# Graph-network chain on one core: the block stage's one-hots written as 32-bit rounded floats, its weights split in two parts

## Time and profile before

| | us |
|---|---|
| median of three runs | 2580.64 |
| the profiled execution's own time | 2578.91 |
| its span, first to last instruction | 2577.2 |
| TensorE matmul busy | 2291.4 (89%) |
| VectorE busy | 1690.3 (66%) |
| ScalarE busy | 922.8 (36%) |
| GpSimd busy | 1375.3 (53%) |
| mean granted TensorE clock, of full speed | 0.88 |

### The profile page before, as it was taken

The page is one execution under the profiler, slowest core; times in us unless marked ns, Lnnn a source line. Parts: engine busy times, 40 slices in busy tenths (PEclk is TensorE's granted clock), DMA queues, the critical chain, the costliest instruction groups (busy, mean ns, idle before and its releaser), DMA issues.

```text
span 2577.2 us, 38097 instructions
## 1 busy us (share of the span) xinstructions
PE 2291.4 (89%) x7759; PEld 1176.1 (46%) x7759; DVE 1690.3 (66%) x4905; ACT 922.8 (36%) x2623; POOL 1375.3 (53%) x1706
## 2 busy tenths in 40 slices
PE   5789088727779999999998999999999999999997
PEld 3457067616655554454444333333333333333335
DVE  8973389939970421104136888888888888888885
ACT  0010077727760000000103444444444444444444
POOL 3886777776666666566504444444444444444440
PEclk7666555656669999999998999999999999999999
DMA  5212100011121211111102333333333333333331
GB/s 194 53 34 50 6 7 2 2 15 15 15 50 23 50 17 15 51 15 15 47 0 92 89 87 86 86 86 86 86 86 86 86 86 86 86 86 86 86 85 40
DMA packets 77939, 146.95 MB, mean 57 GB/s; under 512 B 28688, under 2 KB 41221, under 8 KB 77517
## 3 DMA queue, kind: packets, MB, share of 16 engines
q0 software_dynamic: 51200, 103.93, 17.6%
q1 hardware_dynamic: 23746, 37.13, 4.4%
q10 hardware_dynamic: 2946, 5.28, 0.6%
HBM read 122.74 MB, written 22.82 MB: 56 GB/s over the span
## 4 chain that ended last, share of the span: by engine, by line
PE 70%; POOL 15%; DVE 7%; issue 5%; DMA 2%; DVEq 1%; ACT 0%; ACTq 0%; SPq 0%; POOLq 0%
PE ps L747 25%; POOL pair_table L446 15%; PE ps L735 13%; PE ps L550 10%; PE ps L575 7%; PE ps L736 4%; PE ps L692 3%; PE ps L637 2%; PE ps L719 1%; DVE dense L1108 1%; DVE adj_t L1130 1%; DMA pair_table<-dense 1%; DVE dense L1107 1%; PE ps L669 1%; PE ps L727 1%
## 5 line engine op out<-in xcount | busy, mean ns | idle before, releaser
L747 PE MATMUL ps<-adj_t 128*128 128x512 f32 x1408 | 670.7, 609 | 0.0
L458 POOL DMA_INDIRECT src_table<-st_rec,st_idx x320 | 386.4, 1208 | 273.3 <-DMA st_rec<-records 181.2
L446 POOL DMA_INDIRECT pair_table<-dense x320 | 395.2, 1235 | 150.4 <-issue 96.6
L505 POOL DMA_INDIRECT adj_t<-z_table,adj_t x352 | 340.6, 968 | 182.3 <-issue 85.1
L927 ACT ACTIVATE adj_t<-adj_t 128x128 f32<-128x128 f32 x1056 | 343.3, 388 | 257.6 <-DVE adj_t L1275 257.6
L735 PE MATMUL ps<-wring,adj_t 128*128 128x512 f32 x704 | 371.8, 610 | 2.9 <-DVE adj_t L1249 2.9
L747 PEld LDWEIGHTS ps<-adj_t 128*128 128x128 f32 x1408 | 246.6, 190 | 251.0 <-issue 242.0
L636 PE MATMUL ps<-dense 128*128 128x128 bf16 x512 | 147.0, 287 | 188.4 <-DVE adj_t L1130 119.6
L637 PE MATMUL ps<-dense 128*128 128x128 f32 x1024 | 303.7, 434 | 0.0
L637 PEld LDWEIGHTS ps<-dense 128*128 128x128 f32 x1024 | 249.5, 299 | 19.5
L861 ACT ACTIVATE dense<-dense 128x128 f32<-128x128 bf16 x512 | 157.2, 307 | 248.9 <-DVE dense L1108 238.5
(11 more groups left out here) (208 smaller groups left out, 3083.3 us busy)
## 6 DMA issues: line engine op xcount, KB each, us to landing
src_table<-dense SPq DMA_DIRECT2D x8, 704.0 KB, 7.0
adj_t<-src_table SPq DMA_DIRECT2D x88, 64.0 KB, 1.8
adj_t<-z_table,adj_t POOLq DMA_INDIRECT x352, 3.6
pair_table<-dense POOLq DMA_INDIRECT x320, 2.6
src_table<-st_rec,st_idx POOLq DMA_INDIRECT x320, 2.6
records<-dense SPq DMA_DIRECT2D x1, 5000.0 KB
st_rec<-records POOLq DMA_DIRECT2D x80, 62.5 KB, 2.2
wring<-in_edge_attr SPq DMA_DIRECT2D x2, 1562.5 KB
```

The costliest lines, as they stand in the source:

```text
L446: g.indirect_dma_start(out=pair_tables[h], out_offset=bass.IndirectOffsetOnAxis(ap=rows_i[h][0:EP, j:j + 1].bitcast(u32), axis=0), in_=pai ...
L458: g.indirect_dma_start(out=src_table, out_offset=bass.IndirectOffsetOnAxis(ap=st_idx[0:EP, k, c:c + 1].bitcast(u32), axis=0), in_=st_rec[0 ...
L505: g.indirect_dma_start(out=zg[:, s, c, :], out_offset=None, in_=z_table, in_offset=bass.IndirectOffsetOnAxis(ap=dsti[:, s, c:c + 1].bitcas ...
L747: last = mm(bank[6 + h], oh[:, c, :], msg[:, c, h * D:(h + 1) * D], start=c == 0, stop=c == GROUP - 1)
```

## The change

The type of the four operands of the block products becomes float32r, a 32-bit float rounded for TensorE. VectorE writes both one-hots in it, from the same bf16 row of numbers. The weight of a record is split into a rounded part and the rest, once for each part of the edges, by two chained VectorE instructions after the wait for the table; the rest takes the place of the record's fourth word. ScalarE makes two scaled copies of the destination's one-hot, by the rounded weight and by the rest, and copies the source's one-hot no more. TensorE makes one product of 256 columns (A, and W with the rounded weight) and one of 128 that is accumulated onto W. The ring `sel` takes 4096 words of `dense` where the two before took 3072, and `dense_r` is the same memory as `dense`.

```diff
-        sel_b = dense[:, 0:2 * AB * P].bitcast(bf16).rearrange("p (c k n) -> p c k n", k=2, n=P)
-        sel_f = dense[:, 2 * AB * P:6 * AB * P].rearrange("p (c k n) -> p c k n", k=2, n=P)
+        sel = dense_r[:, 0:8 * AB * P].rearrange("p (c k n) -> p c k n", k=4, n=P)
+        HI_AT = PAIR_AT + PAIR_CHUNKS * PAIR_COLS
+        w_hi = dense_r[:, HI_AT:HI_AT + PAIR_CHUNKS].rearrange("p (h c) -> p h c", h=PARTS)
...
-                    mm(bank[c][:, 0:P], sel_b[:, c, 0, :], sel_b[:, c, 1, :], start=True, stop=True)
-                    mm(bank[c][:, P:2 * P], sel_f[:, c, 0, :], sel_f[:, c, 1, :], start=True, stop=True).then_inc(blk_done, 1)
+                    mm(bank[c][:, 0:2 * P], sel[:, c, 0, :], sel[:, c, 1:3, :].rearrange("p k n -> p (k n)"), start=True, stop=False)
+                    mm(bank[c][:, P:2 * P], sel[:, c, 0, :], sel[:, c, 3, :], start=False, stop=True).then_inc(blk_done, 1)
...
-                    A(sel_f[:, c, 0, :], sel_b[:, c, 0, :], ACT.Copy)
-                    A(sel_f[:, c, 1, :], sel_b[:, c, 1, :], ACT.Copy, scale=dense[:, ds(n * PAIR_COLS + (PAIR_AT + 2), 1)]).then_inc(selw_ready, 1)
+                    A(sel[:, c, 2, :], sel[:, c, 1, :], ACT.Copy, scale=dense_r[:, ds(n + HI_AT, 1)].bitcast(f32))
+                    A(sel[:, c, 3, :], sel[:, c, 1, :], ACT.Copy, scale=dense[:, ds(n * PAIR_COLS + (PAIR_AT + 3), 1)]).then_inc(selw_ready, 1)
...
-            dve.wait_ge(pair_in[0], 16)
+            def split_weights(h):
+                dve.wait_ge(pair_in[h], 16)
+                rec = pair_sb[:, h, :].rearrange("p (c w) -> p c w", w=PAIR_COLS)
+                link(v.tensor_copy(w_hi[:, h, :], rec[:, :, 2]))
+                link(v.tensor_tensor(rec[:, :, 3], rec[:, :, 2], w_hi[:, h, :], ALU.subtract))
+
+            split_weights(0)
...
-                v.tensor_scalar(sel_b[:, c, 0, :], iotab[:, :], dense[:, ds(col, 1)], None, ALU.is_equal)
-                v.tensor_scalar(sel_b[:, c, 1, :], iotab[:, :], dense[:, ds(col + 1, 1)], None, ALU.is_equal).then_inc(sel_ready, 1)
+                v.tensor_scalar(sel[:, c, 0, :], iotab[:, :], dense[:, ds(col, 1)], None, ALU.is_equal)
+                v.tensor_scalar(sel[:, c, 1, :], iotab[:, :], dense[:, ds(col + 1, 1)], None, ALU.is_equal).then_inc(sel_ready, 1)
...
-                    dve.wait_ge(pair_in[p], 16)
+                    split_weights(p)
```

More of the change, by code:

```diff
@@ L72, in build @@
           l2_w, l2_b, w_in_s, w_in_v, wf1, bf1, wf2, bf2, w1_s, w1_v, w2_s, w2_v, out):
-    f32, bf16, i32, u32 = mybir.dt.float32, mybir.dt.bfloat16, mybir.dt.int32, mybir.dt.uint32
+    f32, f32r, bf16, i32, u32 = mybir.dt.float32, mybir.dt.float32r, mybir.dt.bfloat16, mybir.dt.int32, mybir.dt.uint32
     ALU, ACT, AX = mybir.AluOpType, mybir.ActivationFunctionType, mybir.AxisListType
@@ L94, in build @@
         adj = adj_t[:, :].rearrange("p (k n) -> p k n", k=2)
-        dense = sb("dense", [P, NT * D + 2 * KT * N])
+        with nc.sbuf_tensor("dense", [P, NT * D + 2 * KT * N], f32) as dense:
+            pass
+        dense_r = sb("dense_r", [P, NT * D + 2 * KT * N], f32r)
         xb = dense[:, 0:NT * D].rearrange("p (t n) -> p t n", t=NT)
@@ L167, in build @@
         st_rec = sb("st_rec", [P, 2, 4 * SRC_COLS])
-        sel_b = dense[:, 0:2 * AB * P].bitcast(bf16).rearrange("p (c k n) -> p c k n", k=2, n=P)
-        sel_f = dense[:, 2 * AB * P:6 * AB * P].rearrange("p (c k n) -> p c k n", k=2, n=P)
+        sel = dense_r[:, 0:8 * AB * P].rearrange("p (c k n) -> p c k n", k=4, n=P)
+        HI_AT = PAIR_AT + PAIR_CHUNKS * PAIR_COLS
+        w_hi = dense_r[:, HI_AT:HI_AT + PAIR_CHUNKS].rearrange("p (h c) -> p h c", h=PARTS)
+        assert HI_AT + PAIR_CHUNKS <= 10 * 1024
         assert KT * N <= PJ * BUCKETS[0] // 2
```

## The result

The changed kernel takes 2584.47 us (median of 12 runs, 2582.36 to 2587.88). The kernel before, run beside it, takes 2581.16 (12 runs, 2577.28 to 2582.25). The ratio is 1.0018 with a 95% interval of 1.0009 to 1.0026: 3.3 us slower, where 2.2 had been worked out. The profiled execution took 2583.92 us.

What follows compares the result with a forecast made beforehand. Part two of the block stage was taken as paced by VectorE's streams, then its sequencer, then TensorE. 8.4 - 6.8 + 1.0 - 0.4 = +2.2 us gave 2581.1 against the profiled time, 2583 as a median, range 2574 to 2608.

Steps and rivals of the forecast that it cites:

- The slack of part one: Part one of the block stage: 43 us of waiting for the scatter's second table, so changes up to that cost nothing.
- The selects: VectorE's one-hot writes in part two: 33 ns longer each, exposed in half the chunks, +8.4 us, ends 0 and +16.9.
- The hiding of the other half: Third add to next half's first add: streams of 1.45 us stay below the sequencer's 1.47 and 1.82, costing nothing.
- Rivals 3 and 4: Part two: selects cost nothing more, -6.2 us, chance 0.10; or nothing hides and nothing comes back, +18 us, chance 0.15.
- Rival 2: VectorE's selects fall to one element a cycle for the new type, +27 us, 2608; chance 0.07.
- TensorE: Block products at bf16's price, 0.53 us a chunk at most, give back 0.21 us an iteration in part two: -6.8 us.
- Rival 1: TensorE becomes the bound if the narrow product costs f32's four passes: eight passes a chunk, +25 us, 2607; chance 0.18.
- ScalarE: Two scaled copies a chunk in part two, 0.58 us where it has 0.72, hidden behind VectorE, costing nothing.
- Rival 5: GpSimd's transfers in part two hold the longer selects up once more each, +28 us, 2609; chance 0.04.
- the sign of 6.19 us for an iteration: Expected sign that the forecast was right: part two's iterations go from 6.14 to 6.19 us.
- The split: VectorE's copy and subtraction on the weight before part two's first chunk: +1.0 us, ends 0.8 and 2.
- The tail: TensorE's last four chunks after the last select, before the last adds: -0.4 us, ends -0.8 and +0.5.

Runs made afterwards that it cites:

- relief kernel: Kernel before, with only the weighted product and its scaled and plain copies in the rounded type, weight's rest left out, selects still bf16: 2574.0 us, ratio 0.9969.
- silent kernel: Kernel before, with GpSimd's scatter for layer four held back until the block stage is over: 2692.89 us, part two's iterations 6.139 us.
- bf16 kernel: Changed kernel's plan with split weight, two scaled copies and two products, but all block operands in bf16: 2575.48 us, ratio 0.9976 to the kernel before.
- silent changed kernel: Changed kernel, with GpSimd's scatter for layer four held back until the block stage is over: 2693.14 us, part two's iterations 6.199 us.
- three bf16 kernels with several runs: The bf16 kernel, 2575.48 us, and it with the weight split on GpSimd before the scatter, 2576.14, or that begun after VectorE's early work, 2573.79.
- bf16 kernel with an f32 input: The bf16 kernel with the selects reading the row of numbers as f32 instead of bf16: 2584.68 us in a single run, iterations 6.333 us.

## Why the prediction was right, and where it was off

The time (2584.47 for 2583) and the direction were right, but one term was missing, and part of the agreement is luck: the missing term (3.2 us) is larger than the whole forecast change (2.2), and what follows on the stage varies by 7.

- **The slack of part one** was read rightly: 5.75 us more there came out of the wait.
- **The selects**, +8.4 us forecast. 32 ns each, paid in half of the chunks, is 0.256 x 32 = +8.2. The hiding of the other half, which was tight by 0.02 us, held: the two long stretches grew by 0.01 and 0.02. Rivals 3 and 4 fall by this.
- **Rival 2** falls by the 280 ns: the selects keep the rate of line 1268.
- **TensorE**, -6.8 forecast, is -6.4 (6.142 to 5.941 in the relief kernel). The chunk at bf16's price was to be 0.53 us at most; it is 0.43. Rival 1's condition is refuted: a further narrow product adds 0.21 us, weight load included, where the f32 product of the kernel before took 0.53 from its start to the next (702.11 to 702.64). That the 0.20 was TensorE's and not GpSimd's is shown by the silent kernel, which kept it, and there by its two kinds of iteration, 6.18 at the lower clock level and 5.93 at the higher. The records of line 637 were to halve; they went from 421 ns to 308, since a record lasts longer than the time to the next start.
- **ScalarE** is hidden, as the relief and the bf16 kernel show together.
- **GpSimd beside the selects**: this is the step that failed. Rival 5 was set aside because "after the 0.53 the next select starts at 0.17, on time; only the end is late". That is so for the selects of the kernel before, and still so for bf16 ones. For selects at half the rate the next select is on time too, but the add behind the pair isn't: where the first of the two is held up it starts 0.03 to 0.30 late, and it sums to 0.10 us an iteration, 3.2 us. The sum of the prediction put this at nothing; the sign of 6.19 us for an iteration came only in the silent kernel, and beside the transfers it was 6.300. Rival 5's mechanism was real, its size of 28 us nine times too large, and it belonged to the sum as a term with ends instead of to the rivals alone. The Trainium skill, GPSIMD Engine Reference, section Specifications, has the two engines contend when VectorE is in a mode that uses both ports. The silent kernels agree, in that no select of part two lasts longer than 0.29 us in them, of either kind, while beside the transfers both kinds reach 0.70; but only the kind with a 4-byte side passes it on, at the 0.10 us.
- **The split** is 1.38 us for 1.0: the copy lasts 0.38, in line with its row, the subtraction 0.61 and not 0.41, and 0.35 of waiting stands behind it, for which the sum had nothing. The silent changed kernel has the same three durations, so they are not GpSimd's.
- **The tail** is -0.48 for -0.4. The first 20 records after the stage cost 0.37 more in this profile (11.31), which was not in the sum. It is not shown to come from the change: the second profile of the changed kernel has 10.89 there, the kernel before 10.94, and the relief kernel, which also leaves the stage at the lower level, 10.25.

In sum, in this profile: 8.2 - 6.4 + 3.2 = +5.0 (5.27 measured between the first and the last select), then 1.38 - 0.48 = +0.9, and the table 0.49 earlier by chance: +5.4, 5.68 measured. The forecast had +2.2. The two profiled times differ by 5.0 (2578.91 and 2583.92). The medians differ by less, 3.3 and 4.7 in the two comparisons, and the stage does not explain that. What follows on it took 1812.7 us in the profile of before, 1812.0 and 1808.2 in the two of the changed kernel, and 1811 to 1815 in the profiles of the relief kernel and the three bf16 kernels with several runs; what these 7 us are was not pursued.

## What to carry to other kernels

A change of type on TensorE is also one on the engine that writes the operand: here the rounded 32-bit type gave TensorE 6.4 us back and took 8.2 on VectorE, whose rate depended on the widest side of its instruction, and bf16 with the weight in two parts gave the same relief with no slower selects. (What two bf16 parts of the weight do to the accuracy of the sums was not compared.) When one engine's instructions are held up beside another's, a late end with a punctual next start is evidence for that kind of instruction only; the same look is due at the kind that the change brings. When two runs of a stage have equal means, look at the granted clock before taking a cause as absent: here more time at the higher level hid some 1.4 us. And work moved to an idle engine can still hold up its neighbour: the same three GpSimd instructions delayed the scatter's start by 1 us at 12 us and by nothing at 41. Read the end of the path as well as its start: at 41 us the table still came later than in the bf16 kernel, and the gain did not show.

## What the runs showed of the hardware that was not expected

- Products in the rounded 32-bit type are far cheaper than f32 ones. A chunk of a 256-column and a 128-column product takes 0.43 us at the lower level, where the same in bf16 takes 0.32, and each further 128-column product adds 0.21, where an f32 one took 0.53. That is one pass of 0.107 more for the chunk than in bf16. Whether the product or its weight load takes it was not separated.
- Selects of both rates are held up beside GpSimd's transfers, to 0.70 us. At the faster rate everything behind them starts on time. At the slower one the add behind a pair is late by up to 0.30 us where the first of the pair was held up, and on time where only the second was. Why was not settled. That it goes with the rate and not with the bytes written is shown by the bf16 kernel with an f32 input.
- TensorE at 96% busy with rounded products was granted the lower clock level for 235 us, where bf16 and f32 products at 74% had 0.65 and the dense f32 products behind the stage 0.98 at 98% busy. What makes the difference stays open: the rounded products have 128 and 256 columns and the dense ones up to 512, and f32 products of the short shape were not tried at the same busy share.
